# Expert up products of a mixture-of-experts layer with the weights stationary instead of the tokens

## The reference

```
def _L1_ffn_ref(hidden_states, gate_w, w1, w2, w3):   # x [2048,128], w1,w3 [8,128,512], w2 [8,512,128]
    logits = x @ gate_w
    mult, sel = _sparse_mixer_routing(logits)          # the two experts of each token, and their weights
    w = jnp.sum(mult[:, :, None] * (sel[:, :, None] == jnp.arange(E)[None, None, :]), axis=1)
    h = jax.nn.silu(jnp.einsum('th,ehf->etf', x, w1)) * jnp.einsum('th,ehf->etf', x, w3)
    out = jnp.einsum('etf,efh,te->th', h, w2, w)
x = x + _L0_attn_a(norm(x)); x = x + _L0_ffn(norm(x)); x = x + _L0_attn_b(norm(x)); x = x + _L0_ffn(norm(x))
x = x + _L1_attn_a(norm(x)); x = x + _L1_ffn(norm(x)); x = x + _L1_attn_b(norm(x)); x = x + _L1_ffn(norm(x))
```

## Time and profile before

| | |
|---|---|
| median of 3 runs | 1183.82 us (1183.71 to 1185.48) |
| the profiled execution | 1184.85 us, its span 1183.1 us |
| mean granted TensorE clock | 0.906 of full speed |
| first expert stage, slots | from about 755 to 883 us of the span |
| second expert stage, slots | from about 1036 to 1166 us |
| PE busy over the span | 964.7 us, 82% |

### The profile page before, as it was taken

How to read it: one execution, slowest core, us unless ns; L and a number is a source line. 1 busy time by engine, 2 the same in 40 slices (tenths; PEclk the granted TensorE clock), 3 DMA queues, 4 the chain that set the end, 5 groups by cost and what they waited for, 6 DMA issues and landing times. The chain is left out here.

```text
span 1183.1 us, 17682 instructions
## 1 busy us (share of the span) xinstructions
PE 964.7 (82%) x6003; PEld 495.9 (42%) x6003; DVE 808.8 (68%) x1504; ACT 510.1 (43%) x1048; POOL 431.0 (36%) x506
## 2 busy tenths in 40 slices
PE   5497899999999999769867964599983994399993
PEld 3232322322222332346644423366651664156662
DVE  6886989999888770388987976533347786733335
ACT  5344577687877677432012111133334431123333
POOL 3320110011011111236853871266642785146661
PEclk9598999999999899979978996699996997689997
DMA  5843500000000000332101201011112210111114
GB/s 126 176 93 55 108 2 1 1 2 2 1 2 1 2 3 1 137 94 70 40 0 32 68 9 36 15 44 42 43 35 80 63 37 1 38 32 43 43 43 121
DMA packets 50205, 51.47 MB, mean 44 GB/s; under 512 B 7668, under 2 KB 39804, under 8 KB 50108
## 3 DMA queue, kind: packets, MB, share of 16 engines
q1 hardware_dynamic: 45128, 40.11, 13.5%
q0 software_dynamic: 4992, 10.23, 3.2%
HBM read 33.22 MB, written 16.91 MB: 42 GB/s over the span
## 5 line engine op out<-in xcount | busy, mean ns | idle before, releaser
L724 DVE TENSOR_REDUCE mpart<-ps 128x2 f32<-128x1024 f32 (+3 forms) x320 | 324.8, 1061 | 47.6 <-PE ps L775 29.2
L852 ACT ACTIVATE arena<-ps 128x512 f32<-128x512 f32 (+3 forms) x640 | 291.7, 543 | 132.1 <-PE ps L792 131.6
L792 PE MATMUL ps<-arena 51*128 51x512 bf16 (+3 forms) x640 | 175.2, 357 | 13.2 <-DMA arena<-mrow 6.3
L806 PE MATMUL ps<-arena,w 128*32 128x512 f32 (+3 forms) x1280 | 153.4, 551 | 2.8 <-ACT arena L852 2.1
L775 PE MATMUL ps<-arena 51*128 51x512 bf16 (+3 forms) x640 | 141.5, 361 | 12.1 <-DVE mpart L724 5.8
L694 POOL TENSOR_SCALAR_AFFINE_SELECT arena<-arena 128x512 f32<-128x512 f32 x64 | 40.6, 635 | 299.3 <-ACT arena L852 219.9
L1689 ACT ACTIVATE arena<-ps 128x512 f32<-128x512 f32 x78 | 46.6, 597 | 219.4 <-PE ps L1752 161.0
L1096 POOL TENSOR_TENSOR arena<-arena 128x512 f32<-128x512 f32 x96 | 121.0, 1272 | 46.2 <-DVE arena L1148 45.8
L1599 DVE COPY arena<-ps 128x128 f32<-128x128 f32 x78 | 22.8, 292 | 150.6 <-PE ps L1742 137.5
L792 PEld LDWEIGHTS ps<-arena 51*128 51x128 bf16 x640 | 49.3, 94 | 167.5 <-ACT arena L852 130.4
L1148 DVE TENSOR_TENSOR_SCAN arena<-ps,arena 128x512 f32<-128x512 f32 x96 | 118.3, 1253 | 0.4 <-POOL arena L1101 0.4
(11 more groups left out here) (265 smaller groups left out, 1440.5 us busy)
## 6 DMA issues: line engine op xcount, KB each, us to landing
w<-in_w SPq DMA_DIRECT2D x2, 2048.0 KB, 11.0
arena<-results SPq DMA_DIRECT2D x16, 256.0 KB, 5.1
arena<-q_stack SPq DMA_DIRECT2D x8, 384.0 KB
arena<-k_stack SPq DMA_DIRECT2D x8, 384.0 KB
arena<-g_v SPq DMA_DIRECT2D x9, 256.0 KB, 4.5
arena<-r_v SPq DMA_DIRECT2D x9, 256.0 KB, 3.6
arena<-l_v SPq DMA_DIRECT2D x9, 256.0 KB, 3.6
tokens<-arena SPq DMA_DIRECT2D x8, 256.0 KB, 2.4
```

Source lines behind the costliest of these rows:

```text
L724: nc.vector.tensor_reduce(out=mpart[:, 2 * pl:2 * pl + 2, t, kc], in_=ps[:, bank:bank + 2, 0:width], axis=AX.X, op=ALU.max).then_inc(ring_ ...
L792: nc.tensor.matmul(ps[:, n % ST, off:CH], rows(Ks, j % 2, 2 * g + j // 2, kt * P, (kt + 1) * P), rows(Qs, j % 2, 2 * g + j // 2, c * CH + ...
L806: ins = nc.tensor.matmul(ps[32 * j:32 * j + 32, O, off:CH], vg[kt // (NT // 2)][:, kt % (NT // 2), g * GH + j, :], probs[:, u % 2, j, off: ...
L852: nc.scalar.activation(probs[:, n % 2, j[0], off:CH], ps[:, (GH * n + j[0]) % ST, off:CH], ACT.Exp, scale=float(HD) ** -0.5).then_inc(exp_ ...
```

## The change

The stationary operand of the up products is exchanged. ACT copies the slot's 512 columns of `w1` and of `w3` to a fixed place `w13` (held twice), and PE multiplies with 128 of these columns stationary and `xsT` (128 tokens) moving, eight matmuls for each slot in place of two. The result then has the hidden columns on the partitions, so the turns L1760, the tile `hid` and the copy L1695 are gone, and DVE's product goes straight to `hidT`. The register read for `w1` and `w3` moves to ACT; PE still reads the expert for `w2`. The down product of slot s comes one iteration earlier, in iteration s+1.

```
-            hid = take(2 * F).rearrange("p (b f) -> p b f", b=2)
+            w13 = take(2 * 2 * F).rearrange("p (b u f) -> p b u f", b=2, u=2)
 # VectorE
-                    for i in range(ST + 2):
+                    for i in range(ST + 1):
                         ...
-                                dve.wait_ge(hid_turned, i - 1)
-                            nc.vector.tensor_tensor(hid[:, i % 2, :], ps[:, 2 + i % 2, :], act_a[:, i % 2, :],
-                                                    ALU.mult).then_inc(hid_ready, 1)
-                        s = i - 2
+                                dve.wait_ge(down_ready, i - 1)
+                            nc.vector.tensor_tensor(hidT[:, i % 2, :, :].rearrange("p f t -> p (f t)"), ps[:, 2 + i % 2, :],
+                                                    act_a[:, i % 2, :], ALU.mult).then_inc(hid_ready, 1)
+                        s = i - 1
 # ScalarE
-                            nc.scalar.activation(act_a[:, i % 2, :], ps[:, i % 2, :], ACT.Silu).then_inc(silu_out, 1)
-                        s = i - 1
-                        if s >= 0:
-                            act.wait_ge(hid_turned, s + 1)
-                            ...
-                            nc.scalar.copy(hidT[:, s % 2, :, :].rearrange("p f t -> p (f t)"), ps[:, 4 + s % 2, :]).then_inc(hidT_ready, 1)
+                    def take_weights(i):
+                        expert = nc.scalar.value_load(expert_of[0:1, i:i + 1], min_val=0, max_val=E - 1)
+                        if i >= 2:
+                            act.wait_ge(up_ready, i - 1)
+                        nc.scalar.copy(w13[:, i % 2, 0, :], w1[:, expert, :]).then_inc(w_ready, 1)
+                        nc.scalar.copy(w13[:, i % 2, 1, :], w3[:, expert, :]).then_inc(w_ready, 1)
+                    take_weights(0)
+                    for i in range(ST):
+                        if i + 1 < ST:
+                            take_weights(i + 1)
+                        act.wait_ge(up_ready, i + 1)
+                        if i >= 2:
+                            act.wait_ge(hid_ready, i - 1)
+                        nc.scalar.activation(act_a[:, i % 2, :], ps[:, i % 2, :], ACT.Silu).then_inc(silu_out, 1)
 # TensorE
-                    for i in range(ST + 2):
+                    for i in range(ST + 1):
-                            nc.tensor.matmul(ps[:, i % 2, :], xsT[:, i % 2, :], w1[:, expert[i], :], start=True, stop=True)
-                            nc.tensor.matmul(ps[:, 2 + i % 2, :], xsT[:, i % 2, :], w3[:, expert[i], :],
-                                             start=True, stop=True).then_inc(up_ready, 1)
-                        s = i - 1
-                        if 0 <= s < ST:
-                            pe.wait_ge(hid_ready, s + 1)
-                            ...
-                            for f in range(NF):
-                                ins = nc.tensor.transpose(ps[:, 4 + s % 2, f * P:(f + 1) * P], hid[:, s % 2, f * P:(f + 1) * P], ident)
-                            ins.then_inc(hid_turned, 1)
+                            for u in (0, 1):
+                                pe.wait_ge(w_ready, 2 * i + 1 + u)
+                                for f in range(NF):
+                                    ins = nc.tensor.matmul(ps[:, 2 * u + i % 2, f * P:(f + 1) * P], w13[:, i % 2, u, f * P:(f + 1) * P],
+                                                           xsT[:, i % 2, :], start=True, stop=True)
+                            ins.then_inc(up_ready, 1)
                         if i + 1 < ST:
                             turn_x(i + 1)
-                        s = i - 2
+                        s = i - 1
                         if s >= 0:
-                            pe.wait_ge(hidT_ready, s + 1)
+                            pe.wait_ge(hid_ready, s + 1)
```

More of the change, by code:

```diff
@@ L1469, in experts @@
             who_ready, holders_found, rows_known = (sem(f"{name}_{n}") for n in ("who_ready", "holders_found", "rows_known"))
-            stored_tokens, x_turned, xsT_ready, up_ready, silu_out, hid_ready, hid_turned, hidT_ready, down_ready, y_ready = (
-                sem(f"{name}_{n}") for n in ("stored_tokens", "x_turned", "xsT_ready", "up_ready", "silu_out", "hid_ready",
-                                             "hid_turned", "hidT_ready", "down_ready", "y_ready"))
+            stored_tokens, x_turned, xsT_ready, w_ready, up_ready, silu_out, hid_ready, down_ready, y_ready = (
+                sem(f"{name}_{n}") for n in ("stored_tokens", "x_turned", "xsT_ready", "w_ready", "up_ready", "silu_out",
+                                             "hid_ready", "down_ready", "y_ready"))
             gathered = [sem(f"{name}_gathered{i}") for i in range(AHEAD)]
@@ L1683, in _ @@
                     norm.scalar(act)
[L1684 to L1688, removed]
-                            nc.scalar.activation(act_a[:, i % 2, :], ps[:, i % 2, :], ACT.Silu).then_inc(silu_out, 1)
-                        s = i - 1
-                        if s >= 0:
-                            act.wait_ge(hid_turned, s + 1)
-                            if s >= 2:
-                                act.wait_ge(down_ready, s - 1)
-                            nc.scalar.copy(hidT[:, s % 2, :, :].rearrange("p f t -> p (f t)"), ps[:, 4 + s % 2, :]).then_inc(hidT_ready, 1)
+                    def take_weights(i):
[4 more added lines that the diff above has]
+                        nc.scalar.copy(w13[:, i % 2, 1, :], w3[:, expert, :]).then_inc(w_ready, 1)
+                    act.wait_ge(moe_loaded, 48)
+                    act.wait_ge(expert_known, 1)
+                    take_weights(0)
[6 more added lines that the diff above has]
+                        nc.scalar.activation(act_a[:, i % 2, :], ps[:, i % 2, :], ACT.Silu).then_inc(silu_out, 1)
                     for k in (1, 2):
@@ L1750, in _ @@
                                 pe.wait_ge(hid_ready, i - 1)
-                            nc.tensor.matmul(ps[:, i % 2, :], xsT[:, i % 2, :], w1[:, expert[i], :], start=True, stop=True)
-                            nc.tensor.matmul(ps[:, 2 + i % 2, :], xsT[:, i % 2, :], w3[:, expert[i], :],
-                                             start=True, stop=True).then_inc(up_ready, 1)
-                        s = i - 1
-                        if 0 <= s < ST:
-                            pe.wait_ge(hid_ready, s + 1)
-                            if s >= 2:
-                                pe.wait_ge(hidT_ready, s - 1)
-                            for f in range(NF):
-                                ins = nc.tensor.transpose(ps[:, 4 + s % 2, f * P:(f + 1) * P], hid[:, s % 2, f * P:(f + 1) * P], ident)
-                            ins.then_inc(hid_turned, 1)
+                            for u in (0, 1):
[4 more added lines that the diff above has]
+                            ins.then_inc(up_ready, 1)
                         if i + 1 < ST:
                             turn_x(i + 1)
-                        s = i - 2
+                        s = i - 1
                         if s >= 0:
-                            pe.wait_ge(hidT_ready, s + 1)
+                            pe.wait_ge(hid_ready, s + 1)
                             if s >= 1:
```

## The result

The changed kernel takes 1213.92 us (median of 4 runs, 1210.84 to 1218.25), the kernel before beside it 1183.76 us. The ratio is 1.026, 95% interval 1.023 to 1.029: slower by 30 us, where 28 us less were forecast. The profiled execution had 1218.25 us, its span 1216.4.

What follows compares the result with a forecast made beforehand. PE alone was taken to bound the expert stages. Mainly 36 slots by 0.35 us plus stage ends gave -14.15 us a stage, -28.3 for two, from 1183.8 to 1155.5 us; range 1151 to 1168, the forecast's own 1152 to 1160.

Steps and rivals of the forecast that it cites:

- The PE slot: Expert stages: without the four turns, PE's slot falls from 3.16 to 2.81 us, a gain of 0.35.
- The rival with 16 weight loads laid bare: Up products: loads not hidden in a run of 16, slot 4.08 us, 72 us slower, 1256; chance 0.03.
- the ratio of the two figures that the Trainium skill gives: Up products: 16 short matmuls cost 2.5 times 4 long ones, an estimated 4.25 us instead of 1.72.
- ACT: its length: ACT's slot: Silu 0.60, two copies 1.16 to 1.26, register read 0 to 0.6; 1.86 to 2.46 us, under 2.81.
- Costing it at nothing: ACT's new register read and copies add no time, covered by PE's slot of 2.81 us.
- Both rivals that put the pace on ACT: ACT's read or copies set the slot: 1166 (chance 0.13, with POOL or late operand), or slower than before (0.03).
- the one on the slower side: ACT's register read costs over 1.30 us, so slower than before: 1196 at 1.5 us, about 1277 at 2.6; chance 0.03.
- Starts and ends of a stage: Each expert stage's ends: +0.16 first slot, -0.19 second to third up product, +0.08 last up product, -1.59 behind it.
- Does everything else fit under 2.81 us?: Check of DVE, ACT, PE's queue and POOL against the new slot: all were found to fit.
- The line on POOL: POOL's scatter 0.99, gather 0.97 and waits: 2.74 us at most, fits under 2.81 by only 0.07.
- the lines on `xsT` (slack 0.17) and on Silu: DVE's xsT copy starts at t+0.31, PE can use it at 0.84, needed at 1.01; Silu at t+0.20, slack 1.0.
- The last rival: Slot stays near 3.16 us because POOL's indirect DMA pair or a latency is already as long: 1184; chance 0.03.

Runs made afterwards that it cites:

- e1: Changed kernel without the gathers of slots 6 to 38, their rows taken again from the first six slots: 1152.57 us, ratio 0.976 to the kernel before.
- e5: Changed kernel with the scatters replaced by plain DMAs from SyncE's queue to consecutive rows, POOL only gathering: 1148.49 us, ratio 0.971 to the kernel before.
- e14: Changed kernel with POOL issuing a plain DMA to consecutive rows in place of each scatter: 1150.28 us, ratio 0.973 to the kernel before.
- e8: Kernel before the change, with the gathers of slots 6 to 38 left out: 1181.84 us, ratio 0.999 to the kernel before.
- e3: Changed kernel with ACT reading the expert and copying w1 and w3 only for slots 0 and 1: 1179.64 us, ratio 0.998 to the kernel before.
- e18: Changed kernel with one gather in four left out from slot 6 on: 1193.52 us, ratio 1.009 to the kernel before.
- e11: Changed kernel with gathers twelve slots ahead and nothing else changed: 1213.55 us, ratio 1.025 to the kernel before.
- e17: Kernel before the change, with 12 gathers in a row at each stage's start instead of 6: 1189.18 us, ratio 1.006 to the kernel before.
- e16: Changed kernel with 24 gathers in a row at each stage's start instead of 6: 1224.04 us (one run).
- e13: Changed kernel with one slot more of distance, gathers twelve ahead, two PSUM banks each for turned x and down product: 1194.00 us, ratio 1.011 to the kernel before.

## Why the prediction was wrong

- **The PE slot: right.** 2.81 us were forecast; where nothing is held it is 2.79, and the 16 up records take 1.79 in e1, and about that here (814.50 to the next turn at 816.38 is 1.88; in the slot behind it, 817.39 to 819.17, it is 1.78). e1, e5 and e14, in which nothing is held, come to 1148 to 1153 us against the 1155.5 forecast; only e1 has its counterpart without the change (e8). The rival with 16 weight loads laid bare is refuted by the same rows, and with it, for float32 here, the ratio of the two figures that the Trainium skill gives (TensorE: Matmul & The Clock Gate, Back-to-back issue gap).
- **ACT: its length right.** Two copies between SBUF took 0.62 and 0.61 us, 1.23 together where 1.16 to 1.26 was taken, and starting 0.52 apart. Its register read is hidden: the first copy starts at 814.76, 0.05 behind Silu's end (814.11 and 0.60). Taking all of it away (e3) left 8 us of idle PE in 80. Costing it at nothing was wrong beside the holds, though: without it the time was 34 us less, and why stays open. Both rivals that put the pace on ACT fall, the one on the slower side too: the kernel did become slower, but not by it.
- **Starts and ends of a stage: right in kind.** The first three up products start 4.19 and 2.89 apart, where 4.43 (4.27 before and 0.16) and 2.81 were forecast, and from the last one's start to the end of the last copy of `y` is 5.23 us (1193.27 to 1198.50), where 1.80 + 3.64 was forecast:

```profile
755.40 3.70 PE L1761 MATMUL ps<-arena 128*128 128x128 f32 x16 [0.53 <-DVE arena L1600]
...
759.59 2.05 PE L1761 MATMUL ps<-arena 128*128 128x128 f32 x16 [0.38 <-issue]
...
762.48 1.95 PE L1761 MATMUL ps<-arena 128*128 128x128 f32 x16
```

- **"Does everything else fit under 2.81 us?": the step that failed.** Two of its lines did. The line on POOL compared GpSimd's own time, 2.74 us at most, with 2.81 and found that it fits. By the steps in which holds end the pair costs an estimated 2 x 1.44 = 2.88 us (from 808.36 to 814.11, four), more than the new slot and less than the old one of 3.16; the earlier trace rows can't show that, since the record of an indirect DMA ends after 0.97 to 0.99. The sum alone doesn't decide it: e18 had 2.52 for a slot and stalled. What the runs show is the condition, two indirect DMAs a slot with hardly a pause, and the price, 1.97 us in every second slot (4.76 and not 2.79). And the lines on `xsT` (slack 0.17) and on Silu took the latency from PE to the next engine, 0.20 to 0.31, as a constant read from one slot. It isn't: it was 2.5 us in every second slot. The turn of x has to be seen, copied and seen again within PE's own slot, so all but 0.17 us of a delay is paid.
- **A warning stood in the trace before.** In every second slot the copy of `y` came later than in the other, with a wait for PE (columns as above):

```profile
811.50 0.98 POOL L1654 DMA_INDIRECT results<-arena  x1 [1.31 <-DVE arena L1616]
...
817.28 0.29 DVE L1616 COPY arena<-ps 128x128 f32<-128x128 f32 x1 [0.46 <-PE ps L1770]
```

  From the down product's start to its copy it is 1.10 us in the first slot (812.57 to 813.67) and 1.55 in the second (from 815.73). The copy comes 5.78 us after the scatter of 811.50, the first of four indirect DMAs, 4 x 1.445: it is the same hold. Without the gathers (e8) every copy comes 1.10 behind. The old order, with the down product two slots behind, hid that 0.4 us, and e8 shows that it cost nothing.
- **The last rival** (POOL's pair is already as long, the slot stays at 3.16: 1184) named the right resource and had the wrong form: a pace that is held, instead of a stall that grows with the row. Against it stood "POOL works 50 of 80 us", which says nothing of a backlog behind the engine.

Shown: both indirect DMAs are needed, holds end at whole multiples of 1.41 to 1.47 us from the row's start (most often the row's length), they are in the old code too, and the forecast's time appears once the gathers are gone or the scatter is plain. Open: what is backed up in the chip, why it is PE's increments that wait, why PE's read and ACT's work change the cost, and from which length of the row on. A row of six gathers held nothing in the changed kernel (755.40 to 759.59 above falls into one), and in the steady loop the third was enough. In a row of twelve the turn of 762.92, in the eighth gather, was held in e11, while in e17 the up product that Silu takes at 761.50, in the eleventh, was on time. Not tried: a kernel whose slot is held at about 2.9 us, so that GpSimd gets a pause after each pair.

## What to carry to other kernels

Before a kernel is made faster around a pair of indirect DMAs, ask whether GpSimd keeps a pause after each pair in the new period. The length of their records (0.97 to 0.99 us) doesn't tell; here holds counted 1.44 us for each, and even a mean below the period (e18) didn't prevent them. A latency read from one slot can be its minimum: look through the trace for slots in which it is longer, and ask what the new order would pay for it. When an engine waits for another that has long been done, and several increments of it are seen at one moment, look for what a third engine was issuing then.

## What the runs showed of the hardware

- Indirect DMAs of 128 rows of 512 bytes are issued by GpSimd every 1.25 to 1.30 us in a row. PE's semaphore increments that fall due late in such a row are seen late, as a rule together, 1.41 to 1.47 us times a whole number after the row's start: 16.99 us with 12 gathers (7.06 after the turn's start), 34.10 with 24, 5.75 with the four of the loop (2.53 after it), against 0.31 after the turn's start elsewhere. In e16 the last of them came at least 2.8 us after the DMA engines had moved the row's last bytes.
- PE's matmuls themselves pause in a long hold, without a wait that the profile shows. In e13, in the row of 12 gathers, the eight down records of one slot took 3.01 us, not 1.06:

```profile
761.94 0.86 PE L1776 MATMUL ps<-w,arena 128*128 x5
...
763.25 0.48 PE L1776 MATMUL ps<-w,arena 128*128 x2 [0.45 <-issue]
764.68 0.27 PE L1776 MATMUL ps<-w,arena 128*128 x1 [0.95 <-issue]
```

- After a long hold PE resumes at the 1.2 GHz level: in e11 the granted clock is 0.50 from 770.30 to 774.00, and 16 up records take 3.57 us (770.33 to 773.90) in place of 1.79.
- A plain DMA issued by GpSimd takes 0.58 us of it, and beside one gather a slot it caused no hold (e14).
